# Graph network on one core: the last layer's node work moved into its edge pipeline

## The reference, cut to what matters

```python
x = layernorm(x + L0(x))        # mean of neighbours, two products, l2 norm
x = layernorm(x + L1(x))        # product by edge type, weighted segment sum, relu
x = layernorm(x + L2(x))        # five gated rounds, then a two-layer MLP
x = layernorm(x + L3(x))

def L3(x):                      # row, col = src, dst
    e = concatenate([x[row], x[col], edge_attr])
    m = silu(silu(e @ eW1 + eb1) @ eW2 + eb2)
    agg = segment_sum(m, row, num_segments=6250)
    update = silu(concatenate([x, agg]) @ nW1 + nb1) @ nW2 + nb2
    return x + update           # so the norm is taken of 2 x + update
```

## Time and profile before

| What | Value |
| --- | --- |
| median of three runs | 11019.69 us (11015.85 to 11026.41) |
| the profiled execution | 11019.11 us, of which the span is 11017.4 us |
| PE busy | 6360.8 us (58%) |
| DVE busy | 5441.9 us (49%) |
| ACT busy | 2184.5 us (20%) |
| POOL busy | 8098.3 us (74%) |

### The profile page before, as it was taken

How to read it: one execution, slowest core, us unless ns; L and a number is a source line. 1 busy time by engine, 2 the same in 40 slices (tenths; PEclk the granted TensorE clock), 3 DMA queues, 4 the chain that set the end, 5 groups by cost and what they waited for, 6 DMA issues and landing times. The chain is left out here.

```text
span 11017.4 us, 162113 instructions
## 1 busy us (share of the span) xinstructions
PE 6360.8 (58%) x41938; PEld 5788.9 (53%) x41939; DVE 5441.9 (49%) x13456; ACT 2184.5 (20%) x7002; POOL 8098.3 (74%) x8298
## 2 busy tenths in 40 slices
PE   0000000455534445787677767777777688879995
PEld 0000000333333334777677767776777688768884
DVE  8885000444434443555455545554555456645554
ACT  0000000111123331111111111111111133335552
POOL 4777777777777776777777777777777777757773
PEclk9999999766655557888888888887888899989998
DMA  2000000222322233333433343334333433332222
GB/s 64 2 2 2 18 7 7 75 78 76 73 67 58 59 56 87 109 108 108 95 107 109 109 94 108 109 109 95 108 109 108 93 110 111 110 69 60 60 59 48
DMA packets 443846, 835.59 MB, mean 76 GB/s; under 512 B 179843, under 2 KB 260708, under 8 KB 442941
## 3 DMA queue, kind: packets, MB, share of 16 engines
q0 software_dynamic: 329728, 718.19, 25.9%
q1 hardware_dynamic: 113975, 115.67, 3.6%
HBM read 742.64 MB, written 90.68 MB: 76 GB/s over the span
## 5 line engine op out<-in xcount | busy, mean ns | idle before, releaser
L602 POOL DMA_INDIRECT rows<-state_table,idx x4160 | 4081.3, 981 | 1301.3 <-issue 1256.0
L673 DVE TENSOR_TENSOR agg<-agg,l_prod 128x250 f32 (+2 forms) x5824 | 2216.9, 381 | 3291.3 <-PE l_prod L650 1659.5
L650 PE MATMUL l_prod<-onehot,rows 128*128 128x125 f32 x16640 | 2574.8, 318 | 1131.6 <-DMA rows<-state_table,idx 492.7
L650 PEld LDWEIGHTS l_prod<-onehot,rows 128*128 128x128 f32 x16640 | 2397.6, 229 | 1260.3 <-DVE agg L673 994.6
L647 PE MATMUL l_prod<-rows,onehot 128*125 128x130 f32 (+1 forms) x3328 | 759.1, 401 | 2227.8 <-DMA rows<-in_x_dram,idx 1634.5
L647 PEld LDWEIGHTS l_prod<-rows,onehot 128*125 128x125 f32 x3328 | 662.4, 295 | 2303.7 <-issue 1954.9
L300 POOL DMA_INDIRECT slots_table<-rec_stage,row_stage x784 | 825.5, 1053 | 382.1 <-issue 242.8
L1561 POOL DMA_INDIRECT l_gathered<-xcol_table,l_idx x832 | 794.4, 955 | 316.7 <-issue 231.5
L656 DVE TENSOR_TENSOR onehot<-iota_row,rec 128x500 f32<-128x500 f32 x1465 | 986.1, 673 | 14.4 <-PEq L110 14.2
L602 POOL DMA_INDIRECT rows<-in_x_dram,idx x832 | 804.9, 967 | 254.3 <-issue 253.1
L602 POOL DMA_INDIRECT rows<-rel_table,idx x832 | 796.0, 957 | 262.3 <-issue 251.6
(11 more groups left out here) (275 smaller groups left out, 8888.7 us busy)
## 6 DMA issues: line engine op xcount, KB each, us to landing
rows<-state_table,idx POOLq DMA_INDIRECT x4160
rel_table<-l_relrow SPq DMA_DIRECT2D x50, 500.0 KB
state_table<-l_row SPq DMA_DIRECT2D x200, 125.0 KB
slots_table<-rec_stage,row_stage POOLq DMA_INDIRECT x1344, 2.1
rows<-in_x_dram,idx POOLq DMA_INDIRECT x832
rows<-rel_table,idx POOLq DMA_INDIRECT x832
l_gathered<-xcol_table,l_idx POOLq DMA_INDIRECT x832
slots_table<-fill SPq DMA_DIRECT2D x8, 936.0 KB, 41.0
```

The costliest lines, as they stand in the source:

```text
L602: pool.indirect_dma_start(out=K["rows"][:, r, 0:width], out_offset=None, in_=table, in_offset=bass.IndirectOffsetOnAxis(ap=K["idx"][:, r:r ...
L650: last = pe.matmul(p[:, s * SLOT:s * SLOT + LANES], K["rows"][:, r, s * D:(s + 1) * D], oh, start=True, stop=True)
L673: dve.tensor_tensor(into, into, of, ALU.add).then_inc(S.added, 1)
```

## The change

Four things are changed.
- **Late scatters.** LATE goes from 224 to 256 columns. The sort scatters 528 columns of the order by source, and the last round of layer 2 scatters 32.
- **x3 stays on the chip.** In the last round ACT copies x3 transposed into the second half of K["state"], and by row into the second half of K["agg"]. The 50 stores to DRAM are gone.
- **First records first.** In `edge_mlp` SP issues the loads of the first 8 halves ahead of the weights, and no longer waits until both areas are cleared.
- **Node work in the edge pipeline.** `layer3_nodes` is gone. A tile's node work hangs on every fourth half, four tiles behind (`NODE_LAG`): PE two products (l_hidn_ps) at the end of one step and one (l_yn_ps) two steps on, ACT one Silu and one Sqrt, DVE six instructions, SP one store of a tile to the output.

```diff
-LATE_PARTS = 2
-LATE = LATE_PARTS * PART
-LATE_LAYER, LATE_ROUND = 44, 34
+LATE = 256
+LATE_LAYER, LATE_ROUND, LATE_LAST = 44, 34, 32
...
-            for q in range(PARTS - LATE_PARTS):
+            for q in range(-(-NOW_TURNS * PARTS // SC_TURNS)):
...
-                        sp.wait_ge(x3_ok, turn.place_in_round(b, 1) + 1)
-                        sp.dma_start(x3_rows[:, bass.ds(tile, 1), :].rearrange("p t f -> p (t f)"), x3[:, even, :])\
-                            .then_inc(x3_out[even], 16)
...
+            late.load(sp, LATE_LAST)
             turns(sp, LAST, last_body, rounds)
...
-                if rnd < LAST:
-                    late.scatter(pool, LATE_ROUND, 3 + rnd)
+                late.scatter(pool, LATE_ROUND if rnd < LAST else LATE_LAST, 3 + rnd)
...
-                            act.copy(x3t[:, 0:LANES], x3t_ps[:, 0:LANES]).then_inc(x3t_ok, 1)
+                            act.copy(x3t[:, 0:LANES], x3t_ps[:, 0:LANES])
+
+                            act.copy(K["state"][:, bass.ds(back + WIDE, LANES)], x3t_ps[:, 0:LANES]).then_inc(x3t_ok, 1)
+                            act.copy(K["agg"][0:LANES, bass.ds(back + WIDE, D)], x3[:, 1 - odd, :]).then_inc(x3_kept, 1)
...
-        line = Pipeline(HALVES, DEEP, LEAD, LEAD)
+        line = Pipeline(HALVES, DEEP, LEAD, 4 * NODE_LAG - 1)
...
+        def place(i, off, n, back=0):
+
+            k = off // 4 - NODE_LAG - back
+            if off % 4 != n or (i is None and not 0 <= k < TILES):
+                return None
+            return k if i is None else i * (DEEP // 4) + k
...
-            sp.wait_ge(zeroed, 2)
...
+            sp.wait_ge(late.done, 16 * LATE)
+            for j in range(DEEP):
+                load(None, j)
+            sp.wait_ge(zeroed, 1)
...
+                k = place(i, off, 0)
+                if k is not None:
+                    col = node_column(pe, PE, k)
...
+                    pe.matmul(hidn_ps[:, 0:LANES], w1n[:, 0, :], x3t[:, bass.ds(col, LANES)], start=True, stop=False)
+                    pe.matmul(hidn_ps[:, 0:LANES], w1n[:, 1, :], sums[:, bass.ds(col, LANES)], start=False, stop=True)\
+                        .then_inc(hidn_ps_ok, 1)
+                k = place(i, off, 2)
+                if k is not None:
+                    pe.wait_ge(hidn_ok, k + 1)
...
+                    pe.matmul(yn_ps[0:LANES, 0:D], hidn[:, 0:LANES], w2n[:], start=True, stop=True)\
+                        .then_inc(yn_ps_ok, 1)
...
+                k = place(i, off, 0, 1)
+                if k is not None:
+                    norm.deviation(act, K, k)
+                k = place(i, off, 1)
+                if k is not None:
+                    act.wait_ge(hidn_ps_ok, k + 1)
...
+                    act.activation(hidn[:, 0:LANES], hidn_ps[:, 0:LANES], ACT.Silu, bias=b1n[:]).then_inc(hidn_ok, 1)
...
+                k = place(i, off, 1, 1)
...
+                    norm.scaled(dve, x4[:, buf, :], y[:], k).then_inc(x4_ok, 1)
+                k = place(i, off, 3)
...
+                    step(dve.tensor_tensor(y[:], yn_ps[0:LANES, 0:D], b2n[:], ALU.add))
+                    step(dve.scalar_tensor_tensor(y[:], x3_rows[:, bass.ds(col, D)], 2.0, y[:], ALU.mult, ALU.add))
+                    norm.moments(dve, y[:], k)
...
-def layer3_nodes(nc, K, T, n_w1, n_b1, n_w2, n_b2, out):
```

229 lines of the change are left out of this document (76 added, 153 removed).

## The result

The changed kernel takes 10817.39 us (median of four runs, 10811.48 to 10819.02), against 11019.18 for the kernel before: a ratio of 0.9814 (0.9802 to 0.9826). The forecast was 10839 with a range down to 10829, so the direction and the large terms were right and the time lies 22 us under it, 12 us outside the range. The profiled execution took 10819.02 us, of which the span is 10817.2.

A forecast was written before the change was run, and what follows sets the result against it. POOL's gathers were taken to pace the edges, with PE close behind. 11019.1 - 41.1 (sort) + 0.3 (x3) - 10.3 (records first) - 139.1 (old node phase) + 10.2 (drain) = 10839.1 us; range 10829 to 10885.

The forecast's parts named there:

- POOL sets the pace: Edges: POOL's gathers take 5.03 us a half and bound the phase; PE has 0.50 us of slack a half.
- Node work beside the edges at no cost: Edges: each tile's node work on PE, DVE and ACT fits slack and idle stretches; price 0, upper bound 45 us.
- the forecast drain of 10.2 us: End of kernel: after the last sums the last two tiles must drain, +10.2 us, bounds 7 and 16.
- I take 0, by the nearer row: Edges: DVE's extra work does not slow gathers, since layer 1 runs the same norm at a mean of 955 ns; 0.
- a rival of 27: Edges: DVE holds up the gathers by layer 2's 33 ns for each of 832, 27 us, giving 10866; chance 0.05.
- The sort's 41.1: Sort: 32 fewer scatters at 1.285 us each end it 41.1 us earlier; they return hidden behind layer 2's tail.
- the seam's 10.0: Layer 2's last gather to the edges' first: 10.0 us shorter, from records first (-10.3) and x3 (+0.3).
- 0.3 more had been forecast for x3: Layer 2's last tiles: ACT's second x3t copy delays PE's projection, +0.3 us, bounds 0 and 0.9.
- rivals on ACT's switches: Edges: a Sqrt/Silu switch costs twice its load and paces PE, 45 us in all, giving 10884; chance 0.11.
- the returned scatters: Start of edges: the 32 late scatters hold it up and the sort's 41 us come back, giving 10881; chance 0.04.
- the clock: Edges: PE runs at half speed after each table load's stop, 300 us slower, giving 11139; chance 0.02.
- the lost start: Edges: PE or slow late gathers swallow the early first gather, 7.9 us back, giving 10847; chance 0.11.

The follow-up runs named there:

- the experiment: Kernel after, with the edges' one-hots comparing a number row in PSUM with records in SBUF, so one SBUF operand instead of two: 10795.86 us.
- the form with three more DVE instructions a half: Every one-hot made by four TENSOR_SCALAR pieces instead of one TENSOR_TENSOR: 10690.33 us in the kernel after; in the kernel before, on a slow chip, 15420.3 us.

## Why the prediction was wrong by 22 us

- **POOL sets the pace: right.** All that was gained or lost in the edges was on POOL. Its waits for ACT's index copies fell (85.3 to 26.9 us).
- **Node work beside the edges at no cost: right for PE, ACT and DVE.** The six products of a tile start 0.11 us from each other, 0.67 us in all as estimated, ACT's switches fell into idle stretches, the forecast drain of 10.2 us measured 10.1, and the old node phase was -129.0 for -128.9.
- **The step that failed: the sum starts from 11019.1 and has no term for the layers.** It takes for granted, without a reason, that stages which the diff leaves alone cost the same, and prices the removed phase at its own 139.1 us. But that phase held POOL's only tensor copies. Without them each of some 7 thousand DMAs ahead of the edges has a median 7 to 10 ns shorter; the sort was 4.9 us shorter than forecast and the stretch to layer 2's last gather 22.1 us. In the kernel before, taking away the copies alone is worth 6.1 and 18.4 us in these stretches, and 40 us in the median time.
- **"I take 0, by the nearer row": wrong too, and of the other sign.** The edges' gathers are held for 15 us (summed over their median; 13.6 by the experiment), where I had 0 and a rival of 27. Their 7.5 us from the missing copies and these 13.6 make +6.1; the table has +6.4. The two have opposite signs, and that the sum misses the edges by only 6 us is luck. The row I took was a bad witness. In the kernel before 36 of layer 1's 832 gathers start with more than 0.13 us of a one-hot ahead and lie 3.6 us over the median; in layer 2 it is 448 of 4160, and 96.9 us. The 988 ns that I put down to more DVE work and wider rows is such a mean as well: the median of that round is 954. And the holder is not the added norm work, but the one-hots that were there before. The section of the Trainium skill that I cited (Advanced Engine Details and Errata, VectorE Performance Modes) names two-port instructions alone; the rule that fits, two SBUF inputs, is that of the section named with the experiment. What shifts the one-hots onto the starts once the node work is there can only be argued: with DVE's share of it removed the hold stayed (963 ns), and with all of it removed, but the three other parts kept, it was all but gone (a mean of 958 at a median of 955). So it comes from what remains: the node work of PE, ACT and SP, or DVE's waits for it.
- **The sort, the seam, the tail.** The sort's 41.1 measured 46.0, the seam's 10.0 measured 12.7, the first because of the missing copies (they give 6.1 there in the kernel before), the second by the shorter way from load to gather (1.2) and 1.1 us ahead of the phase's start, where 0.3 more had been forecast for x3. Last gather to last sums took 3.1 us more, which no term had. The rivals on ACT's switches, the returned scatters and the clock failed to appear; of the lost start, the run with the weights first leaves open whether a part was lost.
- **The range.** It gave 10 us below the forecast to "a shorter drain, a few us at the seams" and 46 above. With 8224 indirect DMAs on one queue, 1 ns more or less on each is up to 8 us. A range on such a kernel has to leave room for that on both sides.

## What to carry to other kernels

Where one queue sets the pace with thousands of like instructions, compare the median of one of them in every stage before and after: 8 ns on each were worth 40 us here, and in the stage that was changed the mean went the other way. A mean above its median tells of a few long ones, and these have a cause of their own. Keep tensor copies off POOL in a kernel that lives on POOL's indirect DMAs, and look at which DVE instruction runs when a long gather starts; if it reads two SBUF tensors, give it one. Before taking over a form with more instructions, time it on more than one chip.

## What the runs showed of the hardware

- POOL's gathers of 128 rows take 944 to 947 ns (median) in a program without tensor copies on POOL and 952 to 955 in one with them (layer 2's wider rows 946 to 949 and 953 to 957, scatters 958 to 962 and 967 to 971), long before the copies run. The gap to the next, 0.30 us, stays.
- A gather on POOL that starts while a one-hot from two SBUF tensors runs, at least 0.04 us behind its start and with more than 0.13 us of it left, ends 0.82 us after that instruction ends. Over the whole of after the indirect DMAs that lie over their median sum to 249 us of excess; 144 us belong to DMAs that start under the one-hots of the layers and 46 to those under the sort's product of is_tile and rank.
- DVE is held too, but for a shorter time. One-hots keep their 0.67 us beside gathers that run already, and get up to 0.07 us longer where both start together. The TENSOR_SCALAR instructions with one SBUF tensor get longer beside a later part of the DMA: the scaling instruction takes 345 ns, and up to 584 where it starts 0.4 to 0.6 us into one, and the pieces of a one-hot 0.43 us instead of 0.28 at 0.5 to 0.6 us.
- On the chips where the kernel before takes 15000 us, register steps of DVE's and SP's queues that take 40 and 33 ns elsewhere sometimes take 0.7 or 1.4 us: in the trace of the kernel before 441 of DVE's 10205 such steps, 230 of SP's 593 and 2 of ACT's 2498, none on PE or POOL, and none at all in the first trace of the same kernel. These are not the whole: with the fused register steps, of which 362 on DVE are long as well, DVE's come to 0.56 ms of the 3.99 that the execution takes longer. PE also stops between its products without a wait that the profile shows, 421 us ahead of l_prod and 73 ahead of l_nz from 6000 to 8000 us, where the first trace has 1.3 and nothing. In the window of the following rows (timeline of DVE in layer 2) no long register step is recorded; PE makes l_nz there with stops of 0.4 to 1.4 us, and ACT waits 10.6 us for PE:

```profile
7020.08 0.67 DVE L656 TENSOR_TENSOR onehot<-iota_row,rec 128x500 f32<-128x500 f32 x1
7026.09 0.35 DVE L1424 SCALAR_TENSOR_TENSOR l_u<-l_rh,b_n,l_gr 128x125 f32<-128x125 f32 x1 [5.34 <-issue]
7026.35 0.34 DVE L1426 SCALAR_TENSOR_TENSOR l_u<-l_rh,b_n,l_gr 128x125 f32<-128x125 f32 x1
7033.48 2.06 DVE L673 TENSOR_TENSOR agg<-agg,l_prod 128x250 f32 x4 [6.79 <-DMA chunk_col<-chunk_tile_table]
```

  DVE sits idle for 5.34 and 6.79 us there. What makes these chips slower by 36% stays open, and so does why the form with three more DVE instructions a half loses on them.
